# A decoder layer's softmax: row sums into two PSUM banks, a ring of three dots units, the row maximum unrounded

## The reference

```python
dots = jnp.einsum('bhnd,bhmd->bhnm', q, k) * temp
dots = fq_floor(dots)
attn = jax.nn.softmax(dots, axis=-1)
attn = fq_floor(attn)
out = jnp.einsum('bhnm,bhmd->bhnd', attn, v)
```

## Time and profile before

| | |
|---|---|
| time, median of 3 runs | 454.83 us (454.3 to 457.43) |
| the profiled execution | 454.38 us, its span 452.7 us |
| busy: PE, DVE, ACT, POOL | 275.6, 406.2, 347.5, 145.8 us |
| granted PE clock over the span | 0.749 of full; 0.50 in the softmax stage |
| HBM read, written | 7.75 MB, 1.58 MB |

### The profile page before, as it was taken

The page is one execution under the profiler, slowest core; times in us unless marked ns, Lnnn a source line. Parts: engine busy times, 40 slices in busy tenths (PEclk is TensorE's granted clock), DMA queues, the critical chain, the costliest instruction groups (busy, mean ns, idle before and its releaser), DMA issues.

```text
span 452.7 us, 7526 instructions
## 1 busy us (share of the span) xinstructions
PE 275.6 (61%) x1915; PEld 136.0 (30%) x1924; DVE 406.2 (90%) x1299; ACT 347.5 (77%) x792; POOL 145.8 (32%) x322
## 2 busy tenths in 40 slices
PE   4878987888677743333323333179997887275460
PEld 3644433443222210000000000053342775152360
DVE  5878999979799999999999999949986988987987
ACT  2699976789899955999999999955776936547233
POOL 2400000001000001999999999990000005530020
PEclk9899999999655555555555555579999899578687
DMA  7600000000444521699998899694000400000002
GB/s 268 168 1 1 1 0 1 25 23 26 162 163 185 195 107 70 145 203 209 199 195 200 199 202 200 130 197 83 1 1 23 138 0 1 1 0 0 1 0 95
DMA packets 84250, 43.26 MB, mean 96 GB/s; under 512 B 69095, under 2 KB 74487, under 8 KB 84090
## 3 DMA queue, kind: packets, MB, share of 16 engines
q1 hardware_dynamic: 82650, 42.69, 36.9%
q10 hardware_dynamic: 1568, 0.21, 0.3%
HBM read 7.75 MB, written 1.58 MB: 21 GB/s over the span
## 4 chain that ended last, share of the span: by engine, by line
DVE 34%; ACT 31%; PE 18%; issue 13%; ACTq 2%; DMA 1%; DVEq 0%; SPq 0%
ACT mem L975 21%; PE ps L475 18%; DVE mem L1102 6%; ACT mem L925 4%; DVE d_max L1105 4%; DVE mem L1526 3%; ACT mem L909 2%; DVE m L1669 2%; DVE m L1670 2%; DVE mem L1272 1%; DVE mem L1322 1%; ACT mem L945 1%; ACTq L975 1%; DMA mem<-in_x 1%; DVE mem L1533 1%
## 5 line engine op out<-in xcount | busy, mean ns | idle before, releaser
L475 PE MATMUL ps<-mem 64*128 64x256 bf16 (+5 forms) x1180 | 174.5, 345 | 103.3 <-DVE row_max L1360 80.0
L975 ACT ACTIVATE mem<-mem,neg_max 128x256 f32<-128x256 int16 x256 | 125.8, 493 | 8.1 <-DVE neg_max L1101 8.1
L475 PEld LDWEIGHTS ps<-mem 64*128 64x128 bf16 (+3 forms) x1188 | 65.0, 114 | 193.2 <-DVE row_max L1360 108.6
L1360 DVE CUSTOM_DVE_ANT_0 mem<-ps,fold,c 128x256 int16<-128x256 f32 x256 | 110.8, 470 | 0.2 <-DVE fold L1102 0.2
L431 POOL TENSOR_SCALAR mem<-mem,r_now 128x256 int16<-128x256 f32 x176 | 81.4, 482 | 76.3 <-DVE r_now L1101 76.1
L475 PE MATMUL ps<-minus,ones_bf 128*128 128x256 bf16 x383 | 60.4, 308 | 36.2 <-ACT mem L975 9.3
L475 PEld LDWEIGHTS ps<-minus,ones_bf 128*128 128x128 bf16 x383 | 41.9, 110 | 58.4 <-ACT mem L945 12.0
L1272 DVE TENSOR_TENSOR mem<-mem 128x1024 bf16<-128x1024 bf16 x78 | 51.1, 685 | 4.9 <-ACT mem L909 3.0
L925 ACT ACTIVATE mem<-ps,c 128x1024 bf16<-128x1024 f32 x48 | 48.3, 1296 | 1.6 <-PE ps L475 1.6
L975 ACT ACTIVATION_READ_ACCUMULATOR mem<-mem,neg_max x256 | 47.8, 187 | 0.0
L945 ACT ACTIVATE mem<-ps,c 128x1024 int16<-128x1024 f32 x32 | 36.1, 1209 | 10.5 <-DVEq L1306 5.4
(11 more groups left out here) (208 smaller groups left out, 362.4 us busy)
## 6 DMA issues: line engine op xcount, KB each, us to landing
mem<-mem SPq DMA_DIRECT2D x64, 256.0 KB, 2.3
mem<-in_L_attn_w_qkv SPq DMA_DIRECT2D x1, 1536.0 KB, 9.0
mem<-in_x SPq DMA_DIRECT2D x4, 256.0 KB, 4.4
mem<-in_x SPq DMA_DIRECT2D x1, 1024.0 KB, 5.5
out<-mem SPq DMA_DIRECT2D x4, 256.0 KB, 2.2
xattn_matrix<-mem SPq DMA_DIRECT2D x1, 512.0 KB
mem<-in_L_attn_w_out SPq DMA_DIRECT2D x1, 512.0 KB, 5.0
mem<-in_L_ffn_W SPq DMA_DIRECT2D x2, 256.0 KB, 5.1
```

Of the source, the lines that this page charges most:

```text
L475: return te.matmul(o_, l_, r_, start=start, stop=stop)
L975: ins = sc.activation(e_ring[:, u % 4, pos], y_ring[:, u % 4, pos], ACT.Exp, scale=scale_reg, bias=neg_max[:, u % 4, pos:pos + 1], accum_o ...
L1360: ins = ve.tensor_tensor_reduce(y_ring[:, slot, pos], ps[:, 2 * slot + pos // 2, (pos % 2) * N:(pos % 2 + 1) * N], shift, col("g_dots"), - ...
```

## The change

row_sums goes from SBUF to PSUM banks 6 and 7: even groups write to one, odd groups to the other. To free them, the dots of this stage use a ring of three units (CODE_RING) in banks 0 to 5. PE's loop over batches becomes 64 units written out, each of which waits for the codes of the unit three back. ACT waits for neg_max before each unit, and once a group for the reciprocals of the group two back, which had the same bank. row_code is gone: neg_max is the unrounded maximum times minus the scale. The first two units get a neg_max of their own (minus_max), after the first code instruction of the next unit. The minimum over all sums is taken ahead of the last group's reciprocal and r_now. The filler matmuls go to bank 2.

```diff
--- before.py
+++ after.py
@@ -202,13 +202,12 @@
         diag_b = sb("diag_b", [P, 1, P], BF16)
         xw_T = sb("xw_T", [P, 2, D])
         mask = sb("mask", [P, D])
-        row_code = sb("row_code", [P, 2, 8])
         fine_c = sb("fine_c", [P, 4])
         row_inv = sb("row_inv", [P, 2, 8])
         r_now = sb("r_now", [P, 4, 4])
         row_max = sb("row_max", [P, 2, 8])
         neg_max = sb("neg_max", [P, 4, 4])
-        row_sums = sb("row_sums", [P, B * GROUPS * 8])
+        SUM_BANK = 6
         stats = at(199, [TILES, 6], F32)
         mv = at(199.5, [TILES, 2], F32)
         sd = sb("sd", [P, TILES])
@@ -259,6 +258,7 @@
         QKV_RING = 3
         O_RING = 3
         DOT_RING = 4
+        CODE_RING = 3
 
         LN_TURN = {"ln1": 0, "ln2": 1, "ln4": 2, "ln3": 0}
 
@@ -694,17 +694,17 @@
 
             pe.sem_inc(sem("y_ready_u"), 3)
             across_bf(7)
-            with pe.Fori(0, B) as b:
-                for u in range(DOT_UNITS):
-                    if u % 2 == 0:
-                        pe.wait_ge(sem(f"staged_codes{u // 2}"), b * 16 + 16)
-
-                    pe.wait_ge(sem("y_ready_u"), b * DOT_UNITS + u + 1)
-                    dots_unit(u, u % DOT_RING).then_inc(sem("dots_codes_unit"), 1)
+            for unit in range(B * DOT_UNITS):
+                b, u = unit // DOT_UNITS, unit % DOT_UNITS
+                if u % 2 == 0:
+                    pe.wait_ge(sem(f"staged_codes{u // 2}"), b * 16 + 16)
+
+                pe.wait_ge(sem("y_ready_u"), unit + 2)
+                dots_unit(u, unit % CODE_RING).then_inc(sem("dots_codes_unit"), 1)
             pe.wait_ge(sem("exp_done"), B * DOT_UNITS + 2)
-            keep_clock(26, 1)
+            keep_clock(26, 2)
             across(0, diag, 1)
-            keep_clock(18, 1)
+            keep_clock(18, 2)
             pe.wait_ge(sem("attn_scale"), 1)
 
 
@@ -965,16 +965,18 @@
             act.sem_inc(sem("exp_done"), 4)
             scale_reg = act.alloc_register("s_dots_bits")
             act.reg_load(scale_reg, col("s_dots")[0:1].bitcast(I32))
+            act.sem_inc(sem("row_inv"), 2)
             with act.Fori(0, B) as b:
                 for u in range(DOT_UNITS):
-                    unit = b * DOT_UNITS + u
+                    unit, bank = b * DOT_UNITS + u, SUM_BANK + (u // 2) % 2
+                    act.wait_ge(sem("neg_max"), unit + 1)
+                    act.wait_ge(sem("fine"), unit + 1)
                     if u % 2 == 0:
-                        act.wait_ge(sem("neg_max"), b * 4 + u // 2 + 1)
-                    act.wait_ge(sem("fine"), unit + 1)
+                        act.wait_ge(sem("row_inv"), b * GROUPS + u // 2 + 1)
                     for pos in range(4):
                         ins = sc.activation(e_ring[:, u % 4, pos], y_ring[:, u % 4, pos], ACT.Exp,
                                             scale=scale_reg, bias=neg_max[:, u % 4, pos:pos + 1],
-                                            accum_out=row_sums[:, bass.ds(unit * 4 + pos, 1)])
+                                            accum_out=ps[:, bank, bass.ds(b * 16 + u // 4 * 8 + u % 2 * 4 + pos, 1)])
                     ins.then_inc(sem("exp_done"), 1)
 
 
@@ -1353,67 +1355,78 @@
             dve.wait_ge(sem("xbv_rows"), 1)
             dve.sem_inc(sem("y_ready_u"), 1)
 
-            def codes(unit, half, k, heads):
-
-                slot = 2 * half + k
+            def codes(unit, heads):
+
+                half, k, bank = unit // 2 % 2, unit % 2, 2 * (unit % CODE_RING)
                 for pos in heads:
                     ins = ve.tensor_tensor_reduce(
-                        y_ring[:, slot, pos], ps[:, 2 * slot + pos // 2, (pos % 2) * N:(pos % 2 + 1) * N], shift,
+                        y_ring[:, unit % 4, pos], ps[:, bank + pos // 2, (pos % 2) * N:(pos % 2 + 1) * N], shift,
                         col("g_dots"), -3.0e38, ALU.add, ALU.max, row_max[:, half, 4 * k + pos:4 * k + pos + 1])
                 if heads[-1] == 3:
                     ins.then_inc(sem("y_ready_u"), 1)
 
+            def minus_max(unit):
+
+                half, k = unit // 2 % 2, unit % 2
+                dve.wait_ge(sem("y_ready_u"), unit + 5)
+                ts(neg_max[:, unit % 4], row_max[:, half, 4 * k:4 * k + 4], col("ns_dots"), None, ALU.mult)\
+                    .then_inc(sem("neg_max"), 1)
+
             def row_reciprocal(grp, half):
 
                 dve.wait_ge(sem("exp_done"), 2 * grp + 6)
-                ve.reciprocal(row_inv[:, half], row_sums[:, 8 * grp:8 * grp + 8]).then_inc(sem("row_inv"), 1)
+                ve.reciprocal(row_inv[:, half], ps[:, SUM_BANK + grp % 2, grp // 2 * 8:grp // 2 * 8 + 8])\
+                    .then_inc(sem("row_inv"), 1)
 
             def row_scale(grp, half):
 
-                dve.wait_ge(sem("row_inv"), grp + 1)
+                dve.wait_ge(sem("row_inv"), grp + 3)
                 ts(r_now[:, 2 * half:2 * half + 2].rearrange("p u h -> p (u h)"), row_inv[:, half], FINE, None,
                    ALU.mult).then_inc(sem("row_scale"), 2)
 
             def step(grp, half, new, old):
 
-                dve.wait_ge(sem("y_ready_u"), 2 * grp + 6)
                 if new:
                     dve.wait_ge(sem("dots_codes_unit"), 2 * grp + 4 + 2 * STAGES)
-                ts(row_code[:, half], row_max[:, half], WHOLE, -WHOLE, ALU.add, ALU.add).then_inc(sem("row_code"), 1)
-                if new:
                     if old:
                         dve.wait_ge(sem("exp_done"), 2 * grp + 3)
-                    codes(2 * grp + 2, 1 - half, 0, (0,))
-                dve.wait_ge(sem("row_code"), grp + 1)
-                ts(neg_max[:, 2 * half:2 * half + 2].rearrange("p u h -> p (u h)"), row_code[:, half],
-                   col("ns_dots"), None, ALU.mult).then_inc(sem("neg_max"), 1)
+                    codes(2 * grp + 2, (0,))
+                dve.wait_ge(sem("y_ready_u"), 2 * grp + 6)
+                ts(neg_max[:, 2 * half:2 * half + 2].rearrange("p u h -> p (u h)"), row_max[:, half],
+                   col("ns_dots"), None, ALU.mult).then_inc(sem("neg_max"), 2)
                 if new:
-                    codes(2 * grp + 2, 1 - half, 0, (1, 2, 3))
+                    codes(2 * grp + 2, (1, 2, 3))
                 if old:
                     row_reciprocal(grp - 1, 1 - half)
                 if new:
-                    codes(2 * grp + 3, 1 - half, 1, (0,))
+                    codes(2 * grp + 3, (0,))
                 if old:
                     row_scale(grp - 1, 1 - half)
                 if new:
-                    codes(2 * grp + 3, 1 - half, 1, (1, 2, 3))
+                    codes(2 * grp + 3, (1, 2, 3))
 
             groups = B * GROUPS
             dve.wait_ge(sem("dots_codes_unit"), 2 + 2 * STAGES)
-            for k in range(2):
-                codes(k, 0, k, (0, 1, 2, 3))
-            step(0, 0, True, False)
+            codes(0, (0, 1, 2, 3))
+            codes(1, (0,))
+            minus_max(0)
+            codes(1, (1, 2, 3))
+            dve.wait_ge(sem("dots_codes_unit"), 4 + 2 * STAGES)
+            codes(2, (0,))
+            minus_max(1)
+            codes(2, (1, 2, 3))
+            codes(3, (0, 1, 2, 3))
             for grp in range(1, groups - 1):
                 step(grp, grp % 2, True, True)
             step(groups - 1, 1, False, True)
+
+            dve.wait_ge(sem("exp_done"), B * DOT_UNITS + 4)
+            link(ve.tensor_reduce(col("m"), ps[:, SUM_BANK:SUM_BANK + 2, 0:4 * groups], AX.XY, ALU.min))
+            link(ve.reciprocal(col("m"), col("m")))
+            across_send(col("m"), 1, diag, 1)
             row_reciprocal(groups - 1, 1)
             row_scale(groups - 1, 1)
-
-
-            dve.wait_ge(sem("exp_done"), B * DOT_UNITS + 4)
-            link(ve.tensor_reduce(col("m"), row_sums[:], AX.X, ALU.min))
-            link(ve.reciprocal(col("m"), col("m")))
-            across(col("m"), 1, diag, 0, col("x"), 1)
+            across_take(1, 0, col("x"))
             scale_of(col("x"), 1, col("s_attn"), col("g_fine"), over=float(0x7F000000 - (14 << 23)), done="attn_scale")
             link(ts(col("s_av"), col("s_attn"), col("s_qkv"), None, ALU.mult))
             numerator("s_av")
```

## The result

The changed kernel takes 451.60 us (median of 7 runs, 450.91 to 452.65), the one before 455.13 beside it (7 runs, 454.30 to 471.47). The ratio is 0.9919, 95% interval 0.9896 to 0.9942: about 3.7 us faster, where 8.2 were forecast. It leaves out slow executions like the one of 471.47. The time is inside the range, 1% above the forecast, and the direction is right.

What follows compares the result with a forecast made beforehand. The prediction took ACT's exponential pair (0.49 us, 3.93 a group) as the bound, with DVE, POOL and DMA close below. A 3.68 us period over 31 groups saves 7.8, start and end cancelling: 454.38 to 446.6 us, range 444.3 to 455.0.

Steps and rivals of the forecast that it cites:

- The ACT pair: Softmax exponentials: ACTIVATE plus READ_ACCUMULATOR falls from 0.49 to 0.450 us with sums in PSUM, a group from 3.93 to 3.60.
- Rival 1: The sums' destination doesn't matter to ACT; the pair stays 0.49 us and the time is 454.4 us; chance 0.22.
- rival 3: ACT waits between writes to SBUF and PSUM, 94 ns more a pair, 24.1 us in all: 478.5 us; chance 0.08.
- The read's record: Sign of being right: READ_ACCUMULATOR's record on ACT near 145 ns, not 187, with the next ACTIVATE 0.05 us after it.
- The longest of ACT 3.60, DVE 3.63, POOL 3.66 and DMA 3.62 decides: Softmax stage: the largest need per group in us sets the period, taken as 3.68 because four nearly equal resources are coupled.
- Neg_max's extra: DVE, once a softmax group: neg_max adds 0.145 us to the spacing of the code instructions.
- POOL's 0.27 us of idle: POOL idles 0.27 us a group for r_now, then needs 3.66; the idle was to be gone after the change.
- Rival 2: A follower (transposes and stage copies in SP's queue, DMA engines) binds at a 3.80 us period: 450.4 us; chance 0.12.
- The reciprocal from PSUM: DVE's 32 reciprocals, one a group, read the sums from PSUM: 0.05 us more a group, DVE needs 3.63.
- Three units of dots: Matmuls start one unit later; DVE's slack of 0.87 us covers it: costs nothing, up to 0.75 a group without cover.
- Start and end: Softmax stage: 0.7 us gained before the second group's exponentials, 0.7 lost at the end; the two cancel.
- The sum: 31 groups x (3.93 - 3.68) = 7.8 us less, start -0.7, end +0.7: 454.38 - 7.8 = 446.6 us.

Runs made afterwards that it cites:

- sums_sbuf: The changed kernel with the row sums in SBUF again: 454.55 us, ratio 0.9985 to the kernel before.
- neg_1x: The changed kernel with an accumulator on neg_max that nobody reads: 452.57 us, ratio 0.9940 to the kernel before.
- neg_rnow_1x: The changed kernel with accumulators on both neg_max and r_now: 447.89 us, ratio 0.9843 to the kernel before.
- neg_late: The changed kernel with neg_max one code instruction later, no accumulators: 451.45 us, ratio 0.9910 to the kernel before.
- best: neg_rnow_1x with the last group's reciprocal and r_now ahead of the minimum again: 445.82 us, ratio 0.9789 to the kernel before.
- pool_short: The changed kernel with GpSimd's 256 scalings cut from 256 to 64 columns each, zeros placed by three memsets: 445.75 us, one run.

## Why the prediction was off

*The ACT pair* was right: 0.450 taken, 0.45 measured, from a row where PSUM was the source. Rival 1 (the destination doesn't matter) is out by sums_sbuf, where the pair is long again, and rival 3 (ACT waits between two memories) by the step of 0.05. The read's record, a sign that the prediction gave, missed: it went from 187 to 177 ns, not to 145, while the step shrank as forecast. The Trainium skill, page VectorE: DVE Perf Modes, section The TRN2 errata, puts the cost on operations with SBUF as source; here SBUF as destination costs the 0.04 us too.

*"The longest of ACT 3.60, DVE 3.63, POOL 3.66 and DMA 3.62 decides"* failed. DVE and POOL were added up as if each ran alone. Two terms were mis-sized by that. Neg_max's extra was 0.145 and became 0.43, and r_now's 0.03 became 0.085: DVE needs 3.24 + 0.43 + 0.12 + 0.085 = 3.87, over the 3.75 a group that the prediction itself named as the mark of being wrong. And POOL's 0.27 us of idle in the earlier trace rows was taken to vanish with ACT's bound; 0.19 of it stays, because r_now can't be done while POOL works. Rival 2 had the right shape and a period of 3.80 (450.4 us), but named the transposes and the DMA queue, which were not it. The row that should have warned was there: row_code, of neg_max's size, with a mean of 322 ns against 237. I took it out of the sum without asking what it waited for, and what comes next in its place.

*The reciprocal from PSUM*: 0.05 taken, nothing measured (197 ns for 200, step 0.12). *Three units of dots*: nothing, as forecast; DVE sat idle for 0.2 us in all ahead of its 256 code instructions. *row_code*: worth nothing alone, as said.

*Start and end*: -0.7 forecast, -0.66 measured. At the end +0.7 forecast and +0.5 measured against the last exponential; the forecast had the diagonal at 0.25, and it waited for POOL (0.83).

*The sum.* Forecast 31 x 0.25 = 7.8. In the profiled executions the 31 groups gave 2.5 (127.00 us from the first code instruction to the last exponential, 130.18 before, 0.66 of it the start). The spans of the two executions differ by 1.8 us: 3.18 from that stretch, 0.29 from what comes after, less 0.5 at the end and 1.17 by which the stage started late. That start says nothing about the change: the first neg_max varied from 171.95 to 175.30 us over kernels that are equal up to there. With both waits gone the stage gives 5.9 us more, where 5.3 were missing, and 446.6 was forecast where 445.8 to 447.9 came. That these agree is no merit of the forecast: it had the floor of the stage about right (3.63 measured, 3.68 taken), and the changed kernel didn't reach it.

## What to carry to other kernels

When a bound is taken away, the next one need not be the largest busy sum. Here small DVE operations that looked long beside their like were waiting for GpSimd's instruction, and the wait counted in full once nothing hid it. Look for loops too: if GpSimd's next work needs a small DVE result, have that result ready while GpSimd still works, or make it in a form that doesn't wait. Here the wait moved to the next operation when one was freed, so free all of them before judging.

## What the runs showed of the hardware

- A tensor_scalar with an accumulator did not wait for GpSimd: 211 to 217 ns for neg_max against 491, 150 to 156 for r_now against 229 in the changed kernel and 453 in neg_1x. Its read adds nothing to the step: neg_max with the read took 0.55 us from code instruction to code instruction (neg_rnow_1x), as without it before. Which mode it runs in, no run shows.
- The wait needn't end with one GpSimd instruction. Neg_max mostly waited for one, but in three groups of neg_late it took 0.98 us (286.98 to 287.96), past GpSimd's end at 287.28 and let in about the next at 287.73; the diagonal of 128x128 waited past the ends of seven (best, 3.55 us), and past one in the changed kernel (298.92 to 299.75, POOL's unbroken row ending at 299.68). Why an operation isn't let in at the first end is open.
- GpSimd gives way too, a little: where neg_max was let in at 229.80 (neg_late), the GpSimd instruction that began at 229.85 took 0.51 us, not 0.48, and the next started 0.50 later, not 0.455.
- Once ACT had no gap, its records drifted: ACTIVATE 0.79 us and read 0.45 (neg_rnow_1x), 1.1 and 0.8 (pool_short), at an unchanged spacing of 0.45. Spacing is the pace, not the record's length.
